# Finer semaphore waits, a narrower product row and another order of the gates in a four-stage graph kernel

## The reference

```python
x = x + _L0_gnn_ref(_layernorm(x), src, dst, W, attn_l, attn_r, W_res)
x = x + _L0_ffn_ref(_layernorm(x)[None], Wg, bg, W1, b1, W2, b2)[0]
x = x + _L1_gnn_ref(_layernorm(x), W1, b1, W2, b2, edge_index)
x = x + _L1_ffn_ref(_layernorm(x)[None], w_fc, b_fc, w_proj, b_proj, alpha_e, alpha_r)[0]

# _L0_gnn_ref, per head
e = leaky_relu(a1[src] + a2[dst], 0.2)
w = exp(e - segment_max(e, dst)[dst])
out = relu(segment_sum(w * ft[src], dst) / segment_sum(w, dst) + res)

# _L0_ffn_ref
top = argmax(x @ Wg + bg)
out = gelu(x @ W1[top] + b1[top]) @ W2[top] + b2[top]

# gcn_conv, twice, with a relu between
out = segment_sum((x @ W)[src] * dinv[src] * dinv[dst], dst) + b
```

## Time and profile before

| | |
|---|---|
| median of three timed runs | 1021.78 us (1020.6 to 1023.49) |
| the profiled execution | 1026.36 us |
| its span | 1024.5 us |
| TensorE busy | 989.0 us, 97% of the span |
| TensorE weight loads busy | 799.3 us, 78% |
| VectorE busy | 598.0 us, 58% |
| ScalarE busy | 312.9 us, 31% |
| GpSimd busy | 67.5 us, 7% |
| mean granted clock of TensorE | 0.994 |
| chain that ended last: TensorE, VectorE, issue | 89%, 4%, 2% |
| first layers of two expert tiles that follow each other start at | 508.68 and 517.41 us, 8.73 apart |

### The profile page before, as it was taken

How to read it: one execution, slowest core, us unless ns; L and a number is a source line. 1 busy time by engine, 2 the same in 40 slices (tenths; PEclk the granted TensorE clock), 3 DMA queues, 4 the chain that set the end, 5 groups by cost and what they waited for, 6 DMA issues and landing times.

```text
span 1024.5 us, 15870 instructions
## 1 busy us (share of the span) xinstructions
PE 989.0 (97%) x5707; PEld 799.3 (78%) x5707; DVE 598.0 (58%) x1264; ACT 312.9 (31%) x888; POOL 67.5 (7%) x134
## 2 busy tenths in 40 slices
PE   7999999999999999999899999999999999999997
PEld 5777678999999999986566665667997557888884
DVE  7887799999999999995223237541111112333231
ACT  2444353665565566433111121221111110110100
POOL 2100000000000000132222211000000000000000
PEclk9999999999999999999999999999999999999999
DMA  6000010111111111016772539123001005001101
GB/s 160 2 1 1 1 55 4 48 39 38 38 48 46 52 37 37 13 59 248 219 265 86 185 124 287 46 75 118 1 1 46 1 1 171 26 30 31 31 12 51
DMA packets 40017, 69.99 MB, mean 68 GB/s; under 512 B 21074, under 2 KB 24926, under 8 KB 39448
## 3 DMA queue, kind: packets, MB, share of 16 engines
q1 hardware_dynamic: 37321, 58.85, 18.3%
q0 software_dynamic: 2080, 10.23, 3.0%
q10 hardware_dynamic: 559, 0.16, 0.1%
HBM read 50.10 MB, written 19.12 MB: 68 GB/s over the span
## 4 chain that ended last, share of the span: by engine, by line
PE 89%; DVE 4%; issue 2%; ACT 1%; DMA 1%; POOL 0%; ACTq 0%; DVEq 0%; POOLq 0%; SPq 0%
PE O L961 19%; PE pw L1127 15%; PE pc L831 8%; PE pa L1156 7%; PE O L958 6%; PE pw L1189 6%; PE ph L1052 5%; PE py L1073 5%; PE pa L1201 3%; PE pf L796 3%; PE pw L1215 2%; PE pf L831 2%; PE O L898 1%; PE pct L808 1%; PE pt L1117 1%
## 5 line engine op out<-in xcount | busy, mean ns | idle before, releaser
L961 PE MATMUL O<-X,masks 125*125 125x264 f32 x1200 | 277.5, 331 | 0.0
L958 PE MATMUL O<-X,CSR 125*125 125x132 f32 x1080 | 244.1, 226 | 0.0
L961 PEld LDWEIGHTS O<-X,masks 125*125 125x125 f32 x1200 | 220.1, 186 | 0.1
L1779 DVE SCALAR_TENSOR_TENSOR masks<-a2b,NA,CSR 125x375 fp32r<-125x375 f32 (+1 forms) x360 | 212.1, 649 | 6.3 <-PE O L961 4.8
L958 PEld LDWEIGHTS O<-X,CSR 125*125 125x125 f32 x1080 | 203.3, 188 | 0.0
L2040 DVE SCALAR_TENSOR_TENSOR UL<-pw,dinv,UH 125x768 fp32r<-125x768 f32 x20 | 20.4, 1018 | 109.6 <-ACT UH L1513 109.6
L1127 PE MATMUL pw<-W 128*125 128x384 f32 x240 | 80.8, 494 | 1.0 <-ACT W L1506 1.0
L831 PE MATMUL pc<-ohs_a,ohd 125*125 125x512 f16 x375 | 78.6, 349 | 1.6 <-DVE ohs_a L1589 1.6
L1127 PE MATMUL pw<-region,xr_or_h 128*125 128x384 f32 x240 | 77.6, 486 | 0.0
L1127 PEld LDWEIGHTS pw<-region,xr_or_h 128*125 128x125 f32 x240 | 45.0, 188 | 32.1
L1127 PEld LDWEIGHTS pw<-W 128*125 128x125 f32 x240 | 45.0, 191 | 31.8 <-issue 2.8
(11 more groups left out here) (252 smaller groups left out, 1441.8 us busy)
## 6 DMA issues: line engine op xcount, KB each, us to landing
a2b<-a_rows SPq DMA_DIRECT2D x12, 610.4 KB
W<-in_L_ffn_W SPq DMA_DIRECT2D x4, 1152.0 KB
WM<-in_L_ffn_W SPq DMA_DIRECT2D x4, 1152.0 KB
xr_or_h<-in_x SPq DMA_DIRECT2D x10, 336.0 KB
XH<-in_x SPq DMA_DIRECT2D x12, 280.0 KB
z_rows<-region SPq DMA_DIRECT2D x10, 336.0 KB
region<-y_rows SPq DMA_DIRECT2D x10, 336.0 KB
x_rows<-xr_or_h SPq DMA_DIRECT2D x10, 336.0 KB
```

Source lines behind the costliest of these rows:

```text
L958: nc.tensor.matmul(O[0:P, bank, d - d0, 2 * DP:4 * DP], CSR[:, s, d * P:(d + 1) * P], X[:, buf, s, 4:6, :].rearrange("p k d -> p (k d)"), ...
L961: ins = nc.tensor.matmul(O[0:P, bank, d - d0, 0:4 * DP], kept, X[:, buf, s, 0:4, :].rearrange("p k d -> p (k d)"), start=s == 0, stop=s == ...
L1779: nc.vector.scalar_tensor_tensor(masks[:, s, 0:(d1 - d0) * P], a2b[:, buf, d0 * P:d1 * P], NA1[:, s, bass.ds(h, 1)], CSR[:, s, d0 * P:d1 * ...
```

## The change

- DP becomes 65; the buffers keep their size (ROOM = 66), so nothing moves in memory, but the rows of FT, X, T12, ev, both and whole are 65 or 130 wide and lie closer.
- Idle products of 128 columns in TensorE's start: two before the edge lists are turned, three behind it. `turn_projections` comes before step 5 instead of step 3.
- Gates: the waits for the two halves of a copy are taken apart, in `turn_z` and `gates`; gates(0) comes before turn_z(1); ScalarE copies tile 0 before it makes z of tile 1.
- Experts: the same in `turn_slots`, `first_layer` and `copy_slots` (s_xt counts twice a tile); `second_layer` waits for each part of gelu; the last tile's `turn_hidden` stands between the halves of the second layer of the tile before it; s_y counts twice a tile, and the last tile is taken out in halves. Idle products before the first turn: six instead of nine.
- Second graph layer: z of tile 0 in two halves, finer waits in `turn_z` and `weigh`, 26 idle products instead of 24.

```diff
-DP = DH + 2
+DP = DH + 1
+ROOM = DH + 2
...
+                def warm_up(n):
+
+                    for _ in range(n):
+                        nc.tensor.matmul(pf[:, 2, 0:128], ident[:, :], ident[:, :], start=True, stop=True)
+
                 pe.wait_ge(s_ident, 2)
+                warm_up(2)
                 pe.wait_ge(s_ef, 1)
...
+                warm_up(3)
...
-                    if n == 3:
+                    if n == 5:
                         turn_projections()
...
                     for k in range(KF):
+                        if k in (0, 4):
+                            pe.wait_ge(s_ztc3, 2 * t + 1 + k // 4)
                         ins = nc.tensor.matmul(pgt[0:NEXP, t % 2, 0:P], WG[:, k, :], ZT[:, t % 2, k, :],
...
-                    for t in range(NT):
+                    gates(0)
+                    turn_z(1)
+                    for t in range(1, NT):
                         if t + 1 < NT:
                             turn_z(t + 1)
                         gates(t)
-                        if t:
-                            turn_gates(t - 1)
+                        turn_gates(t - 1)
...
-                        ins.then_inc(s_xt, 1)
+                            if k in (3, KF - 1):
+                                ins.then_inc(s_xt, 1)
...
-                        pe.wait_ge(s_xtc, 2 * j + 2)
...
+                            if k in (0, 4):
+                                pe.wait_ge(s_xtc, 2 * j + 1 + k // 4)
...
-                    def second_layer(j):
-
-                        pe.wait_ge(s_hg, MH * j + MH)
+                    def second_layer(j, between=None):
+
                         if j:
                             pe.wait_ge(s_yc, j)
                         for g in range(2):
+                            if g and between:
+                                between()
                             for m in range(MH):
+                                if not g:
+                                    pe.wait_ge(s_hg, MH * j + m + 1)
...
-                        ins.then_inc(s_y, 1)
+                            ins.then_inc(s_y, 1)
...
-                    keep_busy(exact, O[:, 1, 2, :], 9)
+                    keep_busy(exact, O[:, 1, 2, :], 6)
...
-                        turn_hidden(j)
+                        if j < NS - 1:
+                            turn_hidden(j)
...
-                        second_layer(j)
+                        second_layer(j, (lambda: turn_hidden(NS - 1)) if j == NS - 2 else None)
...
-                    keep_busy(exact, pw[:, 1, 1, :], 24)
+                    keep_busy(exact, pw[:, 1, 1, :], 26)
...
+                                if turned is not None and not g and f in (0, 4):
+                                    pe.wait_ge(s_ztc_late, turned + 1 + f // 4)
...
+                    copy_zt(0)
                     z_of(1)
-                    copy_zt(0)
                     evict(H - 1, 1, 2)
...
+                    for g0, g1 in ((0, 1), (1, 2)) if j == NS - 1 else ((0, 2),):
+                        dve.wait_ge(s_y, 2 * j + g1)
...
+                    for lo, hi in ((0, HALF), (HALF, D)) if n == 0 else ((0, D),):
+                        nc.vector.tensor_scalar(Z_late[:, n % 2, lo:hi], XR[:, t, lo:hi], mv[:, t, 0:1], rstd[:, t:t + 1],
+                                                ALU.subtract, ALU.mult).then_inc(s_z_late, 1)
```

60 lines of the change are left out of this document (31 added, 29 removed).

## The result

| | before | after |
|---|---|---|
| median of the timed runs | 1022.95 us (8 runs) | 1018.77 us (8 runs, 1018.41 to 1019.38) |
| ratio, 95% interval | | 0.9957 [0.9946, 0.9968] |
| span of the profiled execution | 1024.5 us | 1016.7 us |
| first layers of two expert tiles, apart | 8.73 us | 8.73 us |

It is faster by 0.4%, and the interval excludes no change, but 1018.77 lies above the range (1009.2 to 1018.0). Two things differ at once. The kernel before ran at 1022.95 beside the changed one, and at 1022.7 to 1023.3 later on, 1.2 above the three runs that the forecast started from. And the gain is 4.2, less than half of what was summed.

What follows compares the result with a forecast made beforehand. TensorE was taken to bound the heads, VectorE close behind, with gaps at five other places. Terms summed to 10.55 us, 8.9 with two clock falls at half; 1021.78 less 8.9 gave 1013 us, range 1009.2 to 1018.

Steps and rivals of the forecast that it cites:

- With six they end near 490.5: gain 0.8: Experts' start: six idle products instead of nine end near 490.5 us, gaining 0.8 us, or 0 at full clock.
- no penalty to see: Heads: rows of X starting off 16-byte steps cost nothing, read from products of 418 columns (357 ns) against 416 (353).
- Start: Kernel start: idle products and earlier turn_projections gain 1.5 us, between 0.8 and 2.15 if the clock comes up early.
- Heads: Heads: four columns fewer on the long product save 1.7 ns, times 1200 pairs, 2.0 us (bounds 0 and 3.0).
- something else: Heads: the short product takes 249 of a pair's 554 cycles, set not by columns but most likely by the next weights.
- Gates: Turn from heads to gates: 2.1 us gained, 0.5 from order and 1.6 from a clock fall that should go.
- Start of the experts: Experts' start: 0.8 us from fewer idle products and 1.45 from finer waits at the first two tiles.
- Rival 1: Clock falls elsewhere: six idle products leave TensorE idle before the first gather, slowing the first layer; 1016.1 us, chance 0.12.
- The finer waits make every gap shorter: All stages: the argument against new clock falls behind gaps, which would add 1.7 us for one fall.
- Weigh: First tile of second graph layer: 0.6 us from halves and finer waits, 1.7 from a clock fall, counted at half.
- The cost of 0 for the gelu turn: Experts' end: turning the last hidden tile earlier gains 0, as the wait moves to VectorE's take_out and stays 1.1 us.
- the 0.4 of the halves: Experts' end: taking out the last tile in halves needs about 0.56 instead of 0.96 us after the last product, gain 0.4.

Runs made afterwards that it cites:

- the gates alone: The kernel before with only the finer waits and new order at the gates, on TensorE and ScalarE: 1019.83 us, ratio 0.997.
- the parts alone: The kernel before with one part of the change each: start 1022.21, narrower rows 1021.76, gates 1019.83, experts' finer waits 1022.87, second graph layer 1023.21 us.
- The runs that mend the experts' start: The changed kernel with nine idle products (1017.11 us), with VectorE's register reads behind the second copies (1017.06 us), and with both (1014.62 us).

## Why the prediction was wrong in size

The stages and their order were right; the sum failed in five places. The largest is the start of the experts, where the step that failed is "With six they end near 490.5: gain 0.8": the idle products were not what the stage waited for. The second is the heads' "no penalty to see".

- **Start (predicted 1.5).** The early rise of the clock is an advantage of some 1.2 in the mean, and the mechanism was right: it comes before 11.0 in all nine traces. But in the kernel before it comes anywhere from 10.1 to 16.4, and the profile showed the latest. The 312 ns that the prediction took for the rate at 1.2 GHz are a mean over a stretch that holds the rise: the six products from 12.83 to 14.91 take 347 each, and the clock rose at 16.43.
- **Heads (2.0, came 0.9).** The price of a column on the long product was right (0.174 a head for four, with aligned rows), and so was "something else" setting the short one; what it is was not run. The step that failed is "no penalty to see", a term put at nothing. The rows it rests on could not show one. The products of 418 columns and those of 416 start on and off the step equally often (at columns 0, 418 and 834 of rows of 1250), so the two forms don't part the two starts, and the 4 ns between 357 and 353 are the wait of the first of them: without the first feature block both forms take 353. Parted by their start, in the trace of before, these products follow each other after 190.3 ns on the step and 190.7 off it. So even the right reading there gives 0.4 ns, and the 2.2 ns of a pair of 260 and 130 columns had to be run. The page "SBUF — State Buffer" of the Trainium skill says in its box on cachelines (section "Door 1: The DMA port swizzle") that each access that crosses to a new 16-byte line pays a penalty, and gives no size; the prediction's estimate from it was a gain of nothing. The trace agrees in direction: the penalty took back 1.2 of 2.1.
- **Gates (2.1, the clock counted at half, 1.3).** The parts came nearly as summed (order 0.7 for 0.5, clock 1.6), but the fall follows the old gap in seven of nine traces, so half was too little: 0.7 + 7/9 x 1.6 is 1.9. The median of the gates alone gives 2.9, with 1.9 to 4.3 in its interval.
- **Start of the experts (2.25, came -0.8 in the two profiles, -0.3 in the mean).** Rival 1 came true, at 1018.77 where it had priced 1016.1. The finer waits work (1.0 to 1.3 of 1.45). The 0.8 for fewer idle products took these products for the last thing that the first turn waits for. Two readings were missed. Nine products at full clock end in time anyway, which the prediction names ("0 if the clock is full there") and still sums at 0.8. And then it is VectorE that is late: in the six traces in which its copy came more than 0.5 us behind TensorE's fourth transpose with the reads ahead of it, it started 5.51 to 5.76 us behind its last routing instruction, right at the end of its reads. So six products could win nothing and opened the 1.02 gap, and behind such a gap (0.86 to 1.02) the first layer stood at half clock in four traces of four. "The finer waits make every gap shorter" was the argument against the rival; it did not hold for the gap that the removed products made.
- **Weigh (0.6 and half of 1.7).** 0.4 came, and the fall was counted in one run of two, when it stands in two of nine traces.

The cost of 0 for the gelu turn, with its reason (VectorE's take_out of the tile before), was right to 0.2 us, and the 0.4 of the halves exact. Added up by the traces, 1.2 + 0.9 + 1.9 - 0.3 + 0 + 0.4 + 0.4 + 2/9 x 1.7 is 4.9, and 4.4 with the -0.8, against 4.2 by the medians with 3.3 to 5.5 in the interval. The medians of the parts alone (0.5, 0.9, 2.9, 0.4 and 0.1, 4.8 together) fit this, but only the gates' is clear of noise. The runs that mend the experts' start bring 1.7 each and 4.1 together by medians, 1.65, 1.07 and 2.83 in their traces.

That the three runs of the forecast's base were 1.2 too fast adds to the distance between 1013 and 1018.77, not to the error of the gain. Still open: why the clock falls in one execution of a program and not in the next, which these runs count but don't explain.

## What to carry to other kernels

One profile shows one draw of the clock. Before a fall is put into a sum, or a cold start, profile the same kernel a few times and count how often each stands there; what a change does to a gap may be worth more than what it does to the work. Before taking filler work away, ask what is late behind it when the clock is full, and look for waits that an engine makes for itself: where the named releaser of an instruction had finished well before the idle time ended, ask the trace for the engine's register instructions in that stretch, which no busy time counts. When rows are narrowed, keep each row's start on its step and only leave the surplus unused.

## What was not expected of the hardware

- VectorE stood 5.7 us without a busy row around four register reads. The reads are 2.5 of it, some 0.6 each; 2.8 to 3.1 us pass, in every trace that has them there, between VectorE's branch ahead of them and the first read, and no run tells why. TensorE's own two reads are 1.3 of the 1.6 that show as "issue"; for the rest it waits for the number.
- A pair of rounded products of 260 and 130 columns runs every 229.1 ns if both rows start on 16 bytes and every 231.3 if they start 8 bytes off; in the long aggregation, products of 416 and 418 columns differ by 0.4 ns between such starts. Sixteen columns more on the short one of the pair change nothing, on the long one they cost 7.0 ns.
- The span of the unchanged program was 1024.5 in one profile and 1017.8 in another. Of these 6.7 us, 2.0 stand in the cold start, 1.6 at the gates, 1.7 at the first weigh and 1.3 behind TensorE's last product.
